# All experts' first matrices loaded at the end of the message stage, the chosen two copied by VectorE

## The chip, the core and the metric

The kernel runs on one core of a Trainium2 chip. The metric is the device time of one execution in microseconds (us), median of three runs. The core has five engines that run their own instruction queues and meet only at semaphores: TensorE (PE; its weight loads are PEld), VectorE (DVE), ScalarE (ACT), GpSimd (POOL) and SyncE (SP), which here does little but issue DMA transfers. Memory next to the engines is SBUF (128 partitions) and PSUM (eight banks for the sums of TensorE).

## What is computed

The input is a graph of 12500 nodes with 256 features and 212500 edges, sorted by target. The first half is one graph attention layer; the second, which the change touches, is a mixture of experts:

```python
def _L0_ffn_ref(x, Wr, br, W1, b1, W2, b2, gamma, beta):    # x: 1 x 12500 x 256
    logits = jnp.mean(x, axis=1) @ Wr + br                   # one row of 8 logits
    routing_weights = jax.nn.softmax(logits, axis=-1)
    ...                                                      # scaled by capacity, softmax again
    top_w, top_i = jax.lax.top_k(rw_tok, 2)
    top_w = jax.nn.softmax(top_w, axis=-1)
    h = gelu(einsum('nd,edf->enf', xf, W1) + b1)             # W1: 8 x 256 x 512
    y = einsum('enf,efd->end', h, W2) + b2                   # W2: 8 x 512 x 256
    out = einsum('ne,end->nd', w_dense, y)
    return _layer_norm(out + x, gamma, beta)
```

The mean over all nodes feeds the router, so all 12500 nodes get the same two experts of the eight. Which two is known only when the last node of the first half is done. The kernel then computes these two experts alone.

## The kernel before, in words

**Stages.** A first stage projects all rows and writes a table. The message stage (119 chunks of 1792 edges, with windows of 128 nodes) gathers rows of the table, forms messages and sums them by one-hot products on TensorE; for each window it stores the new rows (`x_mid`), their normalized form (`xn_rows`) and its transpose (`xn_cols`) to memory. Its last three steps are written out (`ahead_of_last`, `last`, `over_last`), and after them a short tail normalizes and stores the last window. Then comes the expert stage: 25 groups of 512 nodes (the last is short).

**The hand-over on VectorE** (lines 1838 to 1909). After the last window it adds up the column sums (`zcol`), TensorE multiplies them with Wr, and VectorE runs a chain of small operations on one partition: softmax, capacity, softmax again. Each is `link`ed: it raises the semaphore `s_setup` and waits for itself. At `N_PICKED` (line 1880) the indices of the two experts are in `top_ii`. It goes on with the weights of the two (lines 1881 to 1889, `N_TOP`; ScalarE does the exponentials, lines 1339 to 1341), TensorE spreads these over the partitions (line 1143) and VectorE copies them to `wtop`. Then it waits for W1 (line 1894), forms four combinations of W1's blocks (lines 1897 to 1900, `N_COMBOS`), waits for W2 and b2 (line 1902), and scales W2 and b2 with the weights (lines 1903 to 1908, `N_EXPERT`).

**The hand-over on SP** (lines 724 to 768). All its transfers go through one DMA queue (q1). It loads `x_mid` of groups 0 and 1 (`fx`), runs step `last`, waits for its sums, and loads `xn_cols` (as `fxT`) and `xn_rows` (as `fxn`) of both groups. Step `over_last` stores a window. Then:

```python
    sp.wait_ge(s_xn, (total + 2) * 32)      # line 739: all earlier stores of normalized rows have landed
    hold(sp, s_sp_held)
    store_xn(last, 0)                        # line 741
```

`hold` only raises a semaphore by one. Twelve more waits with a hold each follow (lines 742 to 751), for loads long done. Then SP waits for `N_PICKED`, reads the two indices into registers (line 753) and issues, for each expert, two halves of W1 and b1 (lines 757, 759), then for each W2 and b2 (lines 762, 764). Behind that it waits for the last stores (lines 765 to 768) and enters the loop over groups: load of group g+2, store of group g.

**A group** (TensorE from line 1058, ScalarE from 1345, VectorE from 1792 and 1806, POOL from 870). The first layer of a group is a 2x2 block product with seven instead of eight block products, in phases of four matmuls each (x8 instructions in the trace): P1 (line 1072), P2 (1074), P5 (1081), P6 (1085), P7 (1089), P4 (1093), P3 (1097). POOL forms the four combinations of the rows (`fx_c`, lines 878 to 883), VectorE once the four of the weights (`w1_c`). ScalarE copies partial sums to SBUF (lines 1352, 1355, 1358) and applies Gelu with the bias b1 (lines 1362, 1365, 1368, 1371). VectorE adds partial sums in `halves`: c11 after P2, c22 after P7, c12 after P3. The second layer is 64 instructions at line 1106; it waits for `N_EXPERT`. After it VectorE adds the input (`summed`, line 1812) and normalizes (`finished`).

TensorE runs the 24 full groups as a loop of four rounds of six (line 1145), ScalarE as a loop of two groups each; it waits for both b1 before it enters. POOL and VectorE have all groups written out.

**Where things lie.** In the expert stage the tiles of the message stage are used again: `fx`, `w1_sb`, `w2_sb`, `fo` (the output) and `fxT` are parts of `flat_rows`, the place of the gathered rows, which the trace therefore calls `rows`; `hT` and `fxn` are in `msg`, `w1_c` and `fx_c` in `oh`.

## Time and profile before

| | us |
|---|---|
| median of three runs (2863.31 to 2869.16) | 2867.67 |
| the profiled execution | 2866.4 |
| its span in the trace | 2864.6 |
| PE busy | 2295.6 (80%) |
| DVE busy | 2268.6 (79%) |
| ACT busy | 1927.5 (67%) |
| POOL busy | 1679.2 (59%) |

The span is the time between the first and the last instruction of the trace; all times in the text are counted from its start. The first stage ends near 150 us, the message stage near 2190, the expert stage fills the rest. Mean granted TensorE clock over the span: 0.907 of full. In rows from an engine's timeline the columns are start, duration, engine, line, operation, tiles written and read, number of instructions, and in brackets the idle time before with what ended it. SPq is SP's own queue, where DMA issues stand. The granted clock (PEclk) is 1.00 at 2.4 GHz and 0.50 at 1.2 GHz.

### The profile page before, as it was taken

The page shows a single profiled execution, that of the slowest core. Times are in us where ns is not written, and L with a number is a line of the kernel's source. Part 1 is how long each engine was busy: PE and PEld are TensorE (multiplying, and loading weights), DVE is VectorE, ACT ScalarE, POOL GpSimd, SP SyncE. Part 2 cuts the span into 40 slices and gives each one's busy share as a digit, 9 for nine tenths or more (in the row PEclk, how much of TensorE's full clock was granted, in tenths as well). Part 3 has the DMA queues.
Part 4 walks back from the last instruction along what each step waited for, and adds up shares of the span by engine and source line. Part 5 has one row for each costly group of instructions (what it writes and reads, how often), then busy time and mean ns, then how long its engine had stood idle before and what let it go on. Part 6 is the DMA issues. An engine that isn't in the chain of part 4 may idle for free. (4 is left out here: it accounts for less than half of the span.)

```text
span 2864.6 us, 56749 instructions
## 1 busy us (share of the span) xinstructions
PE 2295.6 (80%) x14050; PEld 1864.8 (65%) x14050; DVE 2268.6 (79%) x9465; ACT 1927.5 (67%) x6599; POOL 1679.2 (59%) x1771
## 2 busy tenths in 40 slices
PE   7846778777777778777777777778775999999998
PEld 5635656656656656656566656666664888888887
DVE  5538899899899989999899899899996465565566
ACT  4537778787787778777787787777784445445443
POOL 6767777777777777777777777777750111011110
PEclk9977898999888998989988998988897999999999
DMA  9977666666666666666666666666654122222222
GB/s 324 386 258 210 190 183 190 188 185 187 189 183 187 191 181 189 191 181 190 191 182 189 191 184 185 192 183 188 192 165 130 43 76 88 88 66 81 88 82 75
DMA packets 320818, 489.95 MB, mean 171 GB/s; under 512 B 74158, under 2 KB 226778, under 8 KB 320516
## 3 DMA queue, kind: packets, MB, share of 16 engines
q0 software_dynamic: 79760, 228.10, 30.3%
q1 hardware_dynamic: 240180, 257.44, 28.0%
q8 instruction: 100, 1.64, 0.2%
q14 instruction: 202, 1.65, 0.2%
q10 hardware_dynamic: 576, 1.12, 0.1%
HBM read 394.32 MB, written 92.15 MB: 170 GB/s over the span
## 5 line engine op out<-in xcount | busy, mean ns | idle before, releaser
L860 POOL DMA_INDIRECT rows<-table,idx x1543 | 1489.4, 965 | 481.3 <-issue 405.5
L963 PE MATMUL bank<-msg,oh 128*128 128x260 f32 x3324 | 858.1, 414 | 1.5 <-DVE acc L1703 1.2
L963 PEld LDWEIGHTS bank<-msg,oh 128*128 128x128 f32 x3324 | 678.7, 208 | 201.1 <-ACT xln L1318 23.0
L1210 ACT ACTIVATE msg<-rows,we 128x65 f32<-128x65 f32 x1888 | 474.8, 334 | 0.2
L1022 PE MATMUL bank<-ident_b,ohT 128*128 128x128 bf16 x1666 | 148.1, 257 | 313.0 <-DVE rden L1718 115.1
L1552 DVE TENSOR_TENSOR msg<-rows,bank 128x520 f32<-128x520 f32 x595 | 381.6, 679 | 0.5 <-DVEq L113 0.2
L878 POOL TENSOR_TENSOR oh<-rows 128x256 f32<-128x256 f32 x24 | 17.5, 730 | 593.3 <-PE bank L1093 507.4
L1022 PEld LDWEIGHTS bank<-ident_b,ohT 128*128 128x128 bf16 x1666 | 125.2, 116 | 327.4 <-DVE rden L1716 170.1
L1106 PE MATMUL bank<-rows,msg 128*128 128x256 f32 x1536 | 336.6, 378 | 0.0
L1106 PEld LDWEIGHTS bank<-rows,msg 128*128 128x128 f32 x1536 | 290.3, 189 | 42.4
L1249 ACT ACTIVATE asrc<-rows 128x70 f32<-128x70 f32 x119 | 31.8, 267 | 346.5 <-DMA rows<-table,idx 340.3
L1352 ACT ACTIVATE msg<-bank 128x256 f32<-128x256 f32 x96 | 36.6, 385 | 270.1 <-PE bank L1072 266.9
L1203 ACT ACTIVATE oh_b<-bank 128x896 bf16<-128x896 bf16 x238 | 203.3, 905 | 3.8 <-issue 3.4
L1203 ACT ACTIVATE oh<-bank 128x896 f32<-128x896 bf16 x238 | 201.1, 892 | 0.3 <-ACTq L113 0.2
L1658 DVE TENSOR_REDUCE node_v<-bank 128x70 f32<-128x210 f32 x119 | 44.8, 376 | 158.0 <-PE bank L985 143.3
L985 PE MATMUL bank<-ident,asrc 128*70 128x128 f32 x238 | 53.2, 307 | 143.5 <-ACT asrc L1249 125.9
L1547 DVE TENSOR_SCALAR ohT<-dst_b,node 128x896 bf16<-128x896 int16 x238 | 159.9, 672 | 1.2 <-DVEq L113 0.6
L985 PEld LDWEIGHTS bank<-ident,asrc 128*70 128x70 f32 x238 | 26.0, 144 | 186.1 <-ACT asrc L1249 170.8
L1001 PE MATMUL bank<-wx,xeT 128*128 128x260 f32 x480 | 144.8, 430 | 2.3 <-ACTq L113 1.4
L815 POOL DMA_INDIRECT rows<-in_x_rows,oh x119 | 114.4, 961 | 44.6 <-issue 22.5
L1304 ACT ACTIVATE selfm<-tab_w,ws 128x65 f32<-128x65 f32 x476 | 127.0, 338 | 3.9
L1267 ACT ACTIVATE r_c<-carry,r_f 1x65 f32<-1x65 f32 x476 | 125.1, 333 | 0.0
(250 smaller groups left out, 4876.1 us busy)
## 6 DMA issues: line engine op xcount, KB each, us to landing
dst_b<-dst SPq DMA_DIRECT2D x121, 448.0 KB
rows<-table,idx POOLq DMA_INDIRECT x1543
tab_w<-table SPq DMA_DIRECT2D x120, 134.5 KB
xe<-x_src SPq DMA_DIRECT2D x122, 128.0 KB
x_w<-in_x_rows SPq DMA_DIRECT2D x120, 128.0 KB
xn_rows<-xn SPq DMA_DIRECT2D x120, 128.0 KB
xn_cols<-xn_t SPq DMA_DIRECT2D x120, 128.0 KB
x_mid<-x_o SPq DMA_DIRECT2D x119, 128.0 KB
```

Source lines behind the costliest of these rows:

```text
L815: pool.indirect_dma_start(flat_rows[:, bass.ds(stage(c), D)], None, x, bass.IndirectOffsetOnAxis(ap=x_idx[:, c * TILES + GATHERS:(c + 1) * ...
L860: pool.indirect_dma_start(rows[0:n, slot, t, :], None, table, bass.IndirectOffsetOnAxis(ap=idx[slot][0:n, t:t + 1], axis=0), bounds_check= ...
L963: mm = pe.matmul(psA, oh[:, of, t, :], msg[:, of, t, :], start=(t == 0), stop=(t == TILES - 1))
L1001: mm = pe.matmul(psXR, xeT[:, k, :], wx[:, k, 0:D + H], start=(k == 0), stop=(k == KD - 1))
L1022: mm = pe.transpose(ps[:, c:c + P], ohT[:, s, t, 0:P], ident_b[:, :])
L1106: mm = pe.matmul(psY[q // 2][:, q % 2, :], hT[:, f, q * P:(q + 1) * P], w2_sb[:, e, fk, :], start=(f == 0), stop=(f == 2 * KF - 1))
L1203: ins = act.activation(to[:, i * half:(i + 1) * half, :], psO[i].rearrange("p (t n) -> p t n", n=P), ACT.Copy)
L1210: ins = act.activation(head_cols(msg[:, s, t, :])[:, h, :], head_cols(rows[:, at.slot(), t, 0:HC1])[:, h, :], ACT.Copy, scale=we[:, t, h:h ...
L1267: ins = act.activation(head_cols(r_c[:, :])[:, h, :], head_cols(carry[:, 0:HC1])[:, h, :], ACT.Copy, scale=r_f[:, h:h + 1])
L1304: ins = act.activation(head_cols(selfm[:, :])[:, h, :], head_cols(tab_w[:, at.slot(), 0:HC1])[:, h, :], ACT.Copy, scale=ws[:, h:h + 1])
L1547: return dve.tensor_scalar(ohT[:, s, t, 0:P], dst_b[:, s, :].rearrange("p (t n) -> p t n", n=P)[:, t, :], node[:, s:s + 1], None, ALU.is_e ...
L1552: mark(own, name, lambda: dve.tensor_tensor(msg[:, s, t:t + 2, :].rearrange("p t (h c) -> p t h c", h=H), rows[:, s4, t:t + 2, 0:HC1].rear ...
```

## The change

Five edits.

- **Place.** `w1_sb`, `w2_sb` and `fo` get SBUF of their own. In `flat_rows` there is now, behind `fx`, a tile `w1_all` for the first matrices of all eight experts (16 rows of 512 numbers in each partition, 4.19 MB in all), with `fxT` at the very end.
- **Load.** SP loads `w1_all` in one transfer right after the first `fxT` load, once VectorE and ScalarE have made their last messages (two waits are added for that), ahead of `fxn` of group 0 and of both loads of group 1. It is counted by one semaphore, `s_fw1`. The four loads of W1 halves after the picks are gone.
- **Copy.** At `N_PICKED` VectorE waits for the load, reads each index into a register and copies that expert's matrix to `w1_sb` (`N_CHOSEN`), then forms the four combinations. The weights chain (`N_TOP`) comes behind these.
- **Order in group 0.** TensorE no longer waits for `N_TOP` before the groups: the matmul that spreads the weights (`weights_out`, now into bank 7) stands in group 0 between P7 and P4. VectorE does c11 and c22 of group 0 (`halves_seen`) before it copies the weights and scales W2, and c12 (`halves_ended`) behind.
- **Loop.** TensorE's first six groups are written out, and the loop covers the other three rounds.

```diff
--- before.py
+++ after.py
@@ -315,15 +315,17 @@
         x_turn = -len(x_parts) % x_ring
         narrow = flat_rows[:, EP:2 * EP].bitcast(I16)[:, 0:EP]
         fx = part(flat_rows, 0, 3, QB, D)
-        w1_sb = part(flat_rows, slot_size, 2, KD, F)
-        w2_sb = part(flat_rows, slot_size + n_w, 2, KF, D)
-        fo = part(flat_rows, slot_size + 2 * n_w, 2, QB, D)
-        fxT = part(flat_rows, 3 * slot_size, 3, KD, GROUP)
+        n_all = NE * KD * F
+        w1_all = part(flat_rows, 3 * QB * D, NE, KD, F)
+        fxT = part(flat_rows, RING * slot_size - 3 * KD * GROUP, 3, KD, GROUP)
+        w1_sb = sb("w1_sb", [P, 2, KD, F])
+        w2_sb = sb("w2_sb", [P, 2, KF, D])
+        fo = sb("fo", [P, 2, QB, D])
         HG, PF = GROUP // 2, KF
         assert KD == 2 and KF % 2 == 0 and PF == 4
         w1_c = part(flat_oh, 0, 4, 2, KF // 2, P)
         fx_c = part(flat_oh, 4 * KF * P, 4, HG)
-        assert 3 * QB * D <= slot_size and slot_size + 2 * n_w + 2 * QB * D <= 3 * slot_size
+        assert 3 * QB * D + n_all <= RING * slot_size - 3 * KD * GROUP
 
 
         s_w = sem("s_w")
@@ -348,7 +350,7 @@
         s_mid = sem("s_mid")
         s_xn = sem("s_xn")
         s_fwr = sem("s_fwr")
-        s_fw1 = [[sem(f"s_fw1_{i}_{half}") for half in range(2)] for i in range(2)]
+        s_fw1 = sem("s_fw1")
         s_fb1 = sem("s_fb1")
         s_fw2 = sem("s_fw2")
         s_fx = [sem(f"s_fx{i}") for i in range(3)]
@@ -425,10 +427,11 @@
         N_SETUP = N_DIAG + 2
         N_MEAN = N_SETUP + 2 + 1
         N_PICKED = N_MEAN + 13
-        N_EXP = [N_MEAN + 3, N_PICKED + 2, N_PICKED + 7]
+        N_CHOSEN = [N_PICKED + 1, N_PICKED + 2]
+        N_COMBOS = N_PICKED + 6
+        N_EXP = [N_MEAN + 3, N_COMBOS + 2, N_COMBOS + 7]
         N_TOP = N_EXP[2] + 3
-        N_COMBOS = N_TOP + 5
-        N_EXPERT = N_COMBOS + 4
+        N_EXPERT = N_TOP + 5
         WTOP = 9
 
         pads = [(r, min(P, XO_ROWS - r)) for r in range(N, XO_ROWS, P)]
@@ -730,9 +733,16 @@
             step(last, -2, 0)
             pe2.wait(sp, "agg", last)
             hold(sp, s_sp_held)
-            for g in range(2):
-                load_cols(At(0, 3, 0), g)
-                load_rows(At(0, 3, 0), g, fxn, xn_rows)
+            load_cols(At(0, 3, 0), 0)
+            dve2.wait(sp, MSGS[-1], last)
+            hold(sp, s_sp_held)
+            act2.wait(sp, "msgs", last)
+            hold(sp, s_sp_held)
+            sp.dma_start(w1_all.rearrange("p e k f -> p (e k) f"),
+                         W1.rearrange("e (k p) f -> p (e k) f", p=P)).then_inc(s_fw1, 16)
+            load_rows(At(0, 3, 0), 0, fxn, xn_rows)
+            load_cols(At(0, 3, 0), 1)
+            load_rows(At(0, 3, 0), 1, fxn, xn_rows)
             step(over_last, -2, -1)
             fin_act.wait(sp, "nT", fin)
             hold(sp, s_sp_held)
@@ -752,10 +762,6 @@
             sp.wait_ge(s_setup, N_PICKED)
             picked = [sp.value_load(top_ii[0:1, i:i + 1], min_val=0, max_val=NE - 1) for i in range(2)]
             for i, e in enumerate(picked):
-                for half in range(2):
-                    f = slice(half * F // 2, (half + 1) * F // 2)
-                    sp.dma_start(w1_sb[:, i, :, f], W1[bass.ds(e, 1), :, f].rearrange("o (k p) f -> p (o k) f", p=P))\
-                      .then_inc(s_fw1[i][half], 16)
                 sp.dma_start(b1_sb[:, i, :], b1[bass.ds(e, 1), :].rearrange("o (k p) -> p (o k)", p=P),
                              allow_slow_non_contiguous=True).then_inc(s_fb1, 16)
             for i, e in enumerate(picked):
@@ -1055,7 +1061,7 @@
 
             pe3.credit(pe)
 
-            def group(at, at3):
+            def group(at, at3, between=None):
                 x0, x1 = [fxT[:, at3.slot(), k, 0:HG] for k in range(KD)], [fxT[:, at3.slot(), k, HG:] for k in range(KD)]
 
                 def block_of(i, k, m):
@@ -1068,7 +1074,7 @@
 
                 pe.wait_ge(s_fx[at3.slot()], at3.landed(3))
                 for m in range(PF):
-                    pe.wait_ge(s_fw1[m // 2][m % 2], 16)
+                    pe.wait_ge(s_setup, N_CHOSEN[m // (PF // 2)])
                     pe3.mark(f"P1_{m}", pe.matmul(psAl[m], block_of(0, 0, m), x0[0], start=True, stop=True))
                 for m in range(PF):
                     mm = pe.matmul(psBe[m // 2][:, m % 2, :], block_of(0, 1, m), x0[1], start=True, stop=True)
@@ -1088,6 +1094,8 @@
                     act3.wait(pe, f"u2_{m}", at)
                     pe3.mark(f"P7_{m}", pe.matmul(psAl[m], combo(2, m), fx_c[:, 2, :], start=False, stop=True,
                                                   skip_group_check=True))
+                if between:
+                    between()
                 for m in range(PF):
                     dve4.wait(pe, f"c22_{m}", at)
                     pe3.mark(f"P4_{m}", pe.matmul(psAl[m], block_of(1, 1, m), fx_c[:, 3, :], start=False, stop=True,
@@ -1139,10 +1147,13 @@
             for k in range(KD):
                 mm = pe.matmul(bank[4][0:1, 0:NE], zcol[:, k:k + 1], wr_sb[:, k, :], start=(k == 0), stop=(k == KD - 1))
             mm.then_inc(s_once, 1)
-            pe.wait_ge(s_setup, N_TOP)
-            pe.matmul(bank[5][:, 0:2], ones[0:1, :], rt[0:1, WTOP, 0:2], start=True, stop=True).then_inc(s_once, 1)
-            pe.wait_ge(s_setup, N_TOP + 1)
-            with pe.Fori(0, (GROUPS - 1) // 6) as k:
+            def weights_out():
+                pe.wait_ge(s_setup, N_TOP)
+                pe.matmul(psY[1][:, 0, 0:2], ones[0:1, :], rt[0:1, WTOP, 0:2], start=True, stop=True).then_inc(s_once, 1)
+
+            for j in range(6):
+                group(At(0, 2, j), At(0, 3, j), weights_out if j == 0 else None)
+            with pe.Fori(1, (GROUPS - 1) // 6) as k:
                 for j in range(6):
                     group(At(k * 3, 2, j), At(k * 2, 3, j))
             last_group(At(0, 2, GROUPS - 1), At(0, 3, GROUPS - 1))
@@ -1789,7 +1800,7 @@
                                                                      in1=ft[:, :], op0=ALU.add, op1=ALU.mult))
                     own(names[n + 2])
 
-            def halves(at):
+            def halves_seen(at):
 
                 for j in range(2):
                     pe3.wait(dve, f"P2_{j}", at)
@@ -1799,6 +1810,9 @@
                 for m in range(PF):
                     pe3.wait(dve, f"P7_{m}", at)
                     dve4.mark(f"c22_{m}", dve.tensor_tensor(hT[:, 2 * m + 1, HG:], psAl[m], hT[:, 2 * m + 1, HG:], ALU.add))
+
+            def halves_ended(at):
+
                 for m in range(PF):
                     pe3.wait(dve, f"P3_{m}", at)
                     dve4.mark(f"c12_{m}", dve.tensor_tensor(hT[:, 2 * m, HG:], psGa[m], hT[:, 2 * m, HG:], ALU.add))
@@ -1878,6 +1892,18 @@
             link(dve.max_index(top_i[:, :], rt[:, 8, :], rt[:, 6, :]))
             link(dve.tensor_copy(top_ii[:, :], top_i[:, :]))
             assert done[0] == N_PICKED
+            dve.wait_ge(s_fw1, 16)
+            for i in range(2):
+                e = dve.value_load(top_ii[0:1, i:i + 1], min_val=0, max_val=NE - 1)
+                link(dve.tensor_copy(w1_sb[:, i, :, :].unsqueeze(1), w1_all[:, bass.ds(e, 1), :, :]))
+                assert done[0] == N_CHOSEN[i]
+            a11, a12, a21, a22 = [w1_sb[:, :, k, :].rearrange("p e (h i f) -> p e h i f", i=2, f=P)[:, :, :, i, :]
+                                  for i in range(2) for k in range(KD)]
+            link(dve.tensor_tensor(w1_c[:, 0, :, :, :], a21, a22, ALU.add))
+            link(dve.tensor_tensor(w1_c[:, 1, :, :, :], w1_c[:, 0, :, :, :], a11, ALU.subtract))
+            link(dve.tensor_tensor(w1_c[:, 2, :, :, :], a11, a21, ALU.subtract))
+            link(dve.tensor_tensor(w1_c[:, 3, :, :, :], a12, w1_c[:, 1, :, :, :], ALU.subtract))
+            assert done[0] == N_COMBOS
             softmax(6, 7)
             link(dve.max(rt[:, 8, :], rt[:, 7, :]))
             link(dve.tensor_scalar(rt[:, 14, :], rt[:, 8, :], rt[:, 8, 0:1], None, ALU.subtract))
@@ -1887,18 +1913,9 @@
             link(dve.reciprocal(rt[:, 15, 2:3], rt[:, 15, 1:2]))
             link(dve.tensor_scalar(rt[:, WTOP, 0:2], rt[:, 13, 0:2], rt[:, 15, 2:3], None, ALU.mult))
             assert done[0] == N_TOP
+            halves_seen(At(0, 2, 0))
             dve.wait_ge(s_once, 6)
-            link(dve.tensor_copy(wtop[:, :], bank[5][:, 0:2]))
-            for e in range(2):
-                for half in range(2):
-                    dve.wait_ge(s_fw1[e][half], 16)
-            a11, a12, a21, a22 = [w1_sb[:, :, k, :].rearrange("p e (h i f) -> p e h i f", i=2, f=P)[:, :, :, i, :]
-                                  for i in range(2) for k in range(KD)]
-            link(dve.tensor_tensor(w1_c[:, 0, :, :, :], a21, a22, ALU.add))
-            link(dve.tensor_tensor(w1_c[:, 1, :, :, :], w1_c[:, 0, :, :, :], a11, ALU.subtract))
-            link(dve.tensor_tensor(w1_c[:, 2, :, :, :], a11, a21, ALU.subtract))
-            link(dve.tensor_tensor(w1_c[:, 3, :, :, :], a12, w1_c[:, 1, :, :, :], ALU.subtract))
-            assert done[0] == N_COMBOS
+            link(dve.tensor_copy(wtop[:, :], psY[1][:, 0, 0:2]))
             dve.wait_ge(s_fw2, 64)
             for i in range(2):
                 flat = w2_sb[:, i, :, :].rearrange("p k d -> p (k d)")
@@ -1915,7 +1932,9 @@
                 at = At(0, 2, g)
                 if g:
                     summed(*groups(g - 1), lambda: pe3.wait(dve, "out", at, -1))
-                halves(at)
+                if g:
+                    halves_seen(at)
+                halves_ended(at)
                 if g:
                     finished(*groups(g - 1))
             whole, short = groups(GROUPS - 2), groups(GROUPS - 1, QL)
```

## Rows read from the trace of the kernel before

**Rows 1.** The page: span, and busy time of each engine.

```profile
span 2864.6 us, 56749 instructions
...
PE 2295.6 (80%) x14050; PEld 1864.8 (65%) x14050; DVE 2268.6 (79%) x9465; ACT 1927.5 (67%) x6599; POOL 1679.2 (59%) x1771
```

**Rows 2.** The chain of waits around group 0: start us, us, what.

```profile
2200.74 0.28 SPq L753
...
2207.60 6.44 DMA b_sb<-in_L_ffn_b
...
2222.39 13.86 PE bank L1106 x64
```

**Rows 3.** The chain of waits in a steady group.

```profile
2265.66 1.73 PE bank L1081 x8
...
2269.55 1.28 ACT L1362
...
2274.96 13.86 PE bank L1106 x64
```

**Rows 4.** ScalarE in order of time, group 0.

```profile
2209.25 1.28 ACT L1352 ACT_TABLE_LOAD   x1 [9.25 <-DMA b_sb<-in_L_ffn_b]
```

**Rows 5.** VectorE in order of time, picks and weights.

```profile
2197.79 0.16 DVE L1879 CAST top_ii<-top_i 1x8 int32<-1x8 uint32 x1
...
2208.79 0.69 DVE L1897 TENSOR_TENSOR oh<-rows 128x512 f32<-128x512 f32 x1 [7.21 <-DMA rows<-in_L_ffn_W]
...
2214.14 1.54 DVE L1905 TENSOR_SCALAR rows<-rows,wtop 128x1024 f32<-128x1024 f32 x2 [2.47 <-DMA b_sb<-in_L_ffn_b]
```

**Rows 6.** TensorE in order of time, group 0.

```profile
2209.81 3.28 PE L1074 MATMUL bank<-rows 128*128 128x256 f32 x8
2212.93 1.89 PE L1081 MATMUL bank<-oh 128*128 128x256 f32 x8
```

**Rows 7.** SP's DMA issues in order of time.

```profile
2183.34 0.40 SPq L715 DMA_DIRECT2D rows<-xn_cols  x1
...
2184.87 0.47 SPq L710 DMA_DIRECT2D msg<-xn_rows  x1
2191.26 0.36 SPq L643 DMA_DIRECT2D x_mid<-x_o  x1
...
2193.51 1.60 SPq L613 DMA_DIRECT2D xn_cols<-xn_t  x1
2197.68 0.33 SPq L612 DMA_DIRECT2D xn_rows<-xn  x1
...
2202.04 1.00 SPq L757 DMA_DIRECT2D rows<-in_L_ffn_W  x2
2203.22 0.37 SPq L759 DMA_DIRECT2D b_sb<-in_L_ffn_b  x1
...
2204.88 0.37 SPq L759 DMA_DIRECT2D b_sb<-in_L_ffn_b  x1
```

**Rows 8.** One-microsecond stretches; the heading row names the columns.

```profile
core 0: us, PE busy (x) PEld busy (x) DVE busy (x) ACT busy (x) POOL busy (x), PEclk, DMA share, GB/s
...
2189.00:2190.00 1.00, 0.00 (x0) 0.00 (x0) 0.73 (x3) 0.00 (x0) 0.00 (x0) 0.50 1.05 397
...
2195.00:2196.00 1.00, 0.00 (x0) 0.00 (x0) 0.59 (x4) 0.21 (x1) 0.92 (x3) 0.50 0.34 105
...
2210.00:2211.00 1.00, 1.00 (x4) 0.82 (x3) 0.93 (x3) 0.99 (x3) 0.00 (x0) 0.50 0.85 256
...
2212.00:2213.00 1.00, 1.00 (x5) 0.86 (x4) 0.00 (x0) 0.00 (x0) 0.00 (x0) 0.69 0.92 229
```

**Rows 9.** Landing: fxT issued 2183.34, fxn issued 2184.87, both b1.

```profile
DMA to landing us min/median/max: 5.1/5.1/5.1
...
DMA to landing us min/median/max: 8.0/8.0/8.0
...
DMA to landing us min/median/max: 3.9/4.0/4.2
```

## The prediction, made before the change was run

> **What bounds the kernel now.** I read the page first [rows 1]: no engine is full over the span, so the chain that ended last has to be read stage by stage. The change touches only the hand-over between the message stage and the expert stage, some 40 us of 2864.6. There the chain of waits [rows 2] goes: SP reads the two picked experts at 2200.74, issues their loads, the last of them (b2, issued 2207.60) lands 6.44 us later, and the second layer of group 0 starts at 2222.39. From there to the end it is TensorE without a gap that the change could touch; steady groups have the same chain as group 0, with 9.30 us from P5 (2265.66) to the second layer (2274.96) in the groups where ScalarE swaps its table [rows 3]. So everything is decided by when group 0's second layer starts: 2222.39 plus or minus.
>
> Three things hold group 0 today. TensorE's first product waits for the first W1 half. ScalarE starts only when both b1 vectors have landed: it sits until 2209.25, loads its table for 1.28 us and copies [rows 4]. VectorE adds up its combinations at 2208.79 and scales W2 from 2214.14 [rows 5]. TensorE does P2 in 3.28 us at the half clock and P5 at 2212.93 [rows 6]. SP's queue in the same stretch is [rows 7]; how fast the transfers flow is in the one-microsecond stretches [rows 8], and when they land in [rows 9].
>
> **The change, part by part.**
>
> *Removed:* four W1 issues of SP between the picks and b1. From the first (2202.04) to b1 of that expert (2203.22) is 1.18 us, so twice 1.18 = 2.4 us less ahead of the second b1. Also 1.05 MB less in front of b1, b2 and W2.
>
> *Added on the queue:* one load of 4.19 MB, issued right after the first fxT load of 2183.34, and three loads of 0.52 MB (fxn of group 0, fxT and fxn of group 1) behind it instead of ahead. SP adds two waits that are long fulfilled (VectorE's last messages ended near 2171) and one issue, under 1 us; nobody waits for SP there, since its next work is the x_mid store at 2191.26 [rows 7].
> Price of the load: the first fxT landed at 2183.34 + 5.1 = 2188.4 and the last fxn at 2184.87 + 8.0 = 2192.9 [rows 7, 9], so 1.57 MB took 4.4 us, 355 GB/s, and in the full microsecond 2189 it was 397 GB/s [rows 8]. Between these I take 380 for long rows: 4.19 MB = 11.0 us (11.8 to 10.6). W1 lands at 2188.4 + 11.0 = 2199.4, the last fxn at 2203.9.
> The Trainium skill ("DMA: Bandwidth & Descriptors", section Bandwidth) measures 425 GB/s on a 16 MB load. By that the load would take 9.9 us and the sum would be 1.1 us lower; no row here shows more than 397 over a microsecond.
>
> *VectorE:* the picks are ready at 2197.95 [rows 5], so W1 is awaited 1.5 us. Then twice a register load (SP's takes 0.28 [rows 2], about 0.55 with its checks) and a copy of 128x1024. The trace has no such copy: the W2 scaling does the same size in 0.77 [rows 5]; the bound above is twice that. That gives 2199.4 + 2 x 1.35 = 2202.1, the four combinations at 0.72 end at 2205.0 [rows 5], the moved weights chain at 2207.7 (an estimate of 2.7 us: before, it fitted between the picks at 2197.95 and SP's reading at 2200.74). All of it lies before ScalarE starts, so it costs nothing; if that cover went, it would be the 2205.0 that gates P5. W2's scaling, moved behind group 0's P7 additions, takes 2.4 us beside P4 and P3 (3.5 us), and is hidden too. The spreading matmul moved into group 0 is two tiny instructions, at most 0.6 us at the half clock, in a gap before P4. POOL's four subtractions wait for fxn of group 0 at about 2200.9 and need 2.7 us: hidden.
>
> *Moved, and on the path: SP's wait for its stores.* This is the term that decides. Before it may store the last normalized rows (line 741) SP waits for all stores of the step before (line 739). Those are issued at 2191.26 to 2193.51 on the same queue [rows 7]. Before, they met a nearly empty queue and the last was done by about 2197.0, so the store at 2197.68 followed. Now they stand behind the whole backlog: it lands at 2203.9, its data are through some 1.4 us earlier, the 0.39 MB of stores need 1.3 us at 105 GB/s per 0.34 share [rows 8], and the receipt 0.6: 2204.4, the store of line 741 at 2205.1, 7.4 us later. Behind it in SP are twelve waits with their holds (3.06 us from 2197.68 to the pick at 2200.74 [rows 7, 2]), the picks, b1, W2. So the second b1 is issued at 2204.88 + 7.4 - 2.4 = 2209.9. It lands 4.0 us after its issue (3.9 to 4.2 [rows 9]): ScalarE starts at 2214.1 instead of 2209.25, its table and first copy take 1.28 + 0.4, and P5 starts at 2215.8 instead of 2212.93. W2 is issued from 2210.5 to 2212.7 and lands by 2218.7, before VectorE wants it near 2223.
>
> *Clock.* TensorE was granted the half clock from 2186 until the stretch 2212, where it rose (0.69 in that microsecond) after some 4 us of unbroken work that began near 2208.8 [rows 8]. There the slow time lay under waiting. Now P1 and P2 run near 2200 to 2207, TensorE then idles for 9 us, and P5 and a part of P6 meet the half clock: 4 us of work that would be 2 us, so +1.9 us (bounds 0 and 3.5).
>
> *Six groups written out:* TensorE's loop of four rounds becomes one written out and three. The back edges between rounds show no gap in the chain, nor is the loop's entry on the path; nothing, with 0.5 us either way.
>
> *Sum:* P5 at 2215.8, plus 9.30, plus 1.9 = 2227.0 against 2222.39: +4.6 us. On the profiled execution of 2866.4 us that is 2871.0; the median of the three timed runs, 2867.67, stands 1.3 us higher, so I forecast 2872. A measurement of this kernel can tell about 0.2% (5.7 us) from no change; the sum lies inside.
>
> **Rivals.**
>
> *A. The stores are not held up (the other side).* If the three small stores pass the backlog, line 741 stays at 2197.68. The second b1 is issued at 2202.5 and lands at 2206.6, P5 comes at 2208.4 and the second layer at 2217.7 to 2219.6 depending on the clock: -3.7 us, 2864. With the clock's 1.9 us the second layer starts at 2219.6 plus the hold-up of line 741, so this rival decides where that hold-up is under 2.8 us, line 741 before 2200.5. For it: 2.4 us of issues are gone. Against it: the loads landed in the order of their issue [rows 9], all on one queue. The Trainium skill ("DMA: Bandwidth & Descriptors", section Queues, rings and completion order) says that a later descriptor may finish its write before an earlier one, while starts are in ring order. By the first half of that the gain of 3.7 us would be had; the landings here bear out the second half.
>
> *B. The big load flows slowly.* W1's rows stand 256 KB apart in each partition. Mixed traffic moved 256 GB/s at 0.85 share at 2210 [rows 8]; at 300 GB/s the load takes 14.0 us (+3.0), at 256 16.4 us (+5.4). All terms shift with it: +7.6 to +10.0 us, 2875 to 2878. For it speaks only that the loads of 2184 began slowly, against it the 397.
>
> *C. The load is hidden and the path moves little.* If SP's own pace after the wait is shorter without W1 in front of b1 (3 us to land instead of 4) and the clock rises while P1 and P2 run and holds, 1 + 1.9 us fall away: +1.7 us, 2869.
>
> **How the numbers follow.** Held stores at the expected rate: 0.6, with its own range of +1 to +8 us, about a third of it above 5.7. A: 0.17, of which about a third could read as a gain over 0.2%. B: 0.15, nearly all slower. C: 0.08. Slower by over 0.2%: 0.6 x 0.35 + 0.14, with the uncertainty of the medians 0.36; faster by over 0.2%: 0.07; within: 0.57. Range 2863 to 2879: it takes in A's centre below and B's slow end above.
>
> **What would show it.** Right: the store of line 741 near 2205 and a wait of SP for xn_cols of 6 us or more before it; ScalarE's first table load near 2214; W1 landing about 15 us after its issue; P5 at the half clock; the second layer of group 0 near 2227, and all later groups shifted alike. Wrong: line 741 still at 2197.7 (A), W1 landing after 2203 (B), a group 0 that waits for VectorE's copies or combinations, or any change inside the later groups or the message stage.

## The result and the profile after

Twelve runs of each kernel on the same chip gave medians of 2865.96 us before and 2870.52 us with the change, 4.6 us slower: 1.0017 times as long, with a 95% interval of 1.0010 to 1.0024. One of the runs before fell in the chip's slower state and took 3597.61 us; the ratio leaves it out, and without it the median before is 2865.66 us and the difference 4.9 us. The forecast was 2872 us in a range of 2863 to 2879, with "within 0.2%" as the likeliest outcome.

The profiled execution of the changed kernel took 2870.95 us. The page begins so; it answers to [rows 1], and no engine's busy time moved by more than 6 us:

```profile
span 2869.1 us, 56593 instructions
...
PE 2297.0 (80%) x14050; PEld 1870.5 (65%) x14050; DVE 2274.5 (79%) x9467; ACT 1926.5 (67%) x6599; POOL 1684.5 (59%) x1771
```

The span is 4.5 us longer. To place them I measure from a common point, **the turning**: TensorE's matmuls that turn the last normalized rows, at the end of the message stage. They start at 2192.44 before and at 2193.41 after. So 0.97 us arose earlier. Of these, 0.88 us are there before the change can act: SP's last `x_mid` store ahead of the big load goes out at 2180.46 before and at 2181.34 after. From the turning to the second layer of group 0, both by TensorE's order in time, it is 29.79 us before and 34.08 after: +4.29. From there to the end it is 642.37 and 641.61: -0.76. The three make 4.5 us. "Offset" below is always time since the turning.

SP's DMA issues in order of time, changed kernel (it answers to [rows 7]):

```profile
2184.95 0.38 SPq L741 DMA_DIRECT2D rows<-in_L_ffn_W  x1
2185.37 6.12 SPq L713 DMA_DIRECT2D msg<-xn_rows  x1
2191.54 2.60 SPq L718 DMA_DIRECT2D rows<-xn_cols  x1
2194.18 1.31 SPq L713 DMA_DIRECT2D msg<-xn_rows  x1
2196.64 0.89 SPq L646 DMA_DIRECT2D x_mid<-x_o  x1
...
2199.26 0.39 SPq L616 DMA_DIRECT2D xn_cols<-xn_t  x1
2206.55 0.33 SPq L615 DMA_DIRECT2D xn_rows<-xn  x1
...
2210.89 1.00 SPq L765 DMA_DIRECT2D b_sb<-in_L_ffn_b  x2
```

The store that was on line 741 before (now `store_xn` at 2206.55) comes 13.14 us after the turning instead of 5.24: it was held 7.9 us. What held it stands in the table of waits of SP, changed kernel (engine and line, what was waited for, us in total, times, longest), and the landing of the big load in the view of line 741:

```profile
SPq L456 <- DMA xn_cols<-xn_t: 5.9, 1, 5.9
```

```profile
DMA to landing us min/median/max: 15.4/15.4/15.4
```

The load issued at 2184.95 landed at 2200.35. The three loads behind it kept the DMA engines busy until 2205; the last of them, issued at 2194.18, landed 10.4 us later, at 2204.58. One-microsecond stretches (columns as in [rows 8]):

```profile
2191.00:2192.00 1.00, 0.00 (x0) 0.00 (x0) 0.82 (x3) 0.00 (x0) 0.00 (x0) 0.50 1.05 410
2197.00:2198.00 1.00, 0.00 (x0) 0.00 (x0) 0.86 (x6) 0.00 (x0) 0.00 (x0) 0.50 1.03 381
2203.00:2204.00 1.00, 1.00 (x4) 0.34 (x2) 0.97 (x2) 0.00 (x0) 1.00 (x2) 0.50 1.10 365
2204.00:2205.00 1.00, 1.00 (x3) 0.82 (x3) 1.00 (x1) 0.00 (x0) 0.92 (x2) 0.50 0.55 165
2205.00:2206.00 1.00, 1.00 (x4) 0.81 (x3) 0.96 (x2) 0.00 (x0) 0.67 (x1) 0.50 0.01 4
2206.00:2207.00 1.00, 1.00 (x4) 0.82 (x3) 0.93 (x3) 0.00 (x0) 0.00 (x0) 0.50 0.00 0
2207.00:2208.00 1.00, 1.00 (x6) 0.81 (x5) 0.93 (x3) 0.00 (x0) 0.00 (x0) 1.00 0.39 135
2210.00:2211.00 1.00, 0.00 (x0) 0.00 (x0) 0.37 (x2) 0.00 (x0) 0.00 (x0) 0.71 0.00 0
2219.00:2220.00 1.00, 1.00 (x3) 0.77 (x3) 0.00 (x0) 0.38 (x1) 0.00 (x0) 0.50 0.96 344
2220.00:2221.00 1.00, 1.00 (x5) 0.82 (x4) 0.00 (x0) 0.40 (x2) 0.00 (x0) 0.67 1.06 384
```

The DMA share is full until 2204 and next to empty from 2205; SP is released at 2205.75 (2199.26 + 6.49 in the chain below) and issues its store at 2206.55. The clock reached full speed at 2207, while P1 and P2 ran, and was back at the half clock from 2211, after TensorE had gone idle. The chain of waits around group 0, changed kernel (it answers to [rows 2]):

```profile
2199.26 6.49 DMA xn_cols<-xn_t
...
2211.50 2.14 DMA b_sb<-in_L_ffn_b
...
2215.64 3.75 PE bank L1087 x8
2219.39 2.42 PE bank L1091 x8
2221.81 1.73 PE bank L1095 x8
2223.53 0.31 PE bank L1152 x2
...
2227.66 13.81 PE bank L1114 x64
```

Ahead of this piece the chain runs through SP's own issues, the 6.12, 2.60 and 1.31 us above; then come the very stores that SP waits for. The loads of the chosen matrices are gone from it. L1087 is P5 and L1091 is P6; in the next group they take 1.73 and 1.74 us. And VectorE in order of time:

```profile
2201.23 0.69 DVE L1898 COPY w_sb<-rows 128x1024 f32 x1 [3.02 <-DMA rows<-in_L_ffn_W]
2202.71 1.23 DVE L1898 COPY w_sb<-rows 128x1024 f32 x1 [0.79 <-DVE w_sb L1898]
2203.97 1.11 DVE L1902 TENSOR_TENSOR oh<-w_sb 128x512 f32<-128x512 f32 x1
...
2206.98 0.69 DVE L1905 TENSOR_TENSOR oh<-w_sb,oh 128x512 f32<-128x512 f32 x1
```

The first matrices are ready for TensorE earlier than before (combinations done at offset 14.3 against 19.2). P1 and P2 use that, and then TensorE has to stop: P5 needs ScalarE's first copies, and ScalarE is without b1.

### The profile page after: what moved, and what is told of

It reads as the page before. It is cut to its first block and busy times, and to the rows that moved or that the text cites. A ratio compares the mean times of both kernels' runs of the same rounds, so it can differ in the third digit from the quotient of the medians.

```text
span 2869.1 us, 56593 instructions
## 1 busy us (share of the span) xinstructions
PE 2297.0 (80%) x14050; PEld 1870.5 (65%) x14050; DVE 2274.5 (79%) x9467; ACT 1926.5 (67%) x6599; POOL 1684.5 (59%) x1771
## 5 line engine op out<-in xcount | busy, mean ns | idle before, releaser
L1114 PE MATMUL bank<-w_sb,msg 128*128 128x256 f32 x1536 | 335.4, 379 | 0.0
L1114 PEld LDWEIGHTS bank<-w_sb,msg 128*128 128x128 f32 x1536 | 291.8, 190 | 39.7
```

Source lines behind the costliest of these rows:

```text
L1114: mm = pe.matmul(psY[q // 2][:, q % 2, :], hT[:, f, q * P:(q + 1) * P], w2_sb[:, e, fk, :], start=(f == 0), stop=(f == 2 * KF - 1))
```

## The experiments

They ran on other chips, on which the message stage is longer (3280 and 3330 us for the kernel before), so each ratio is against the kernel before on the same chip, and offsets are from each run's own turning.

**1. The picks ahead of the wait for the stores.** SP reads the picks and issues b1, W2 and b2 before the last two stores.

```diff
             step(over_last, -2, -1)
...
+            sp.wait_ge(s_setup, N_PICKED)
+            picked = [sp.value_load(...) for i in range(2)]
+            ... b1, W2, b2 ...
             sp.wait_ge(s_xn, (total + 2) * 32)
             store_xn(last, 0)
-            sp.wait_ge(s_setup, N_PICKED)
-            picked = [sp.value_load(...) for i in range(2)]
-            ... b1, W2, b2 ...
```

> The changed kernel, but SP reads the picks and issues b1, W2 and b2 before it waits for the stores of the last-but-one window. Theory (SP is held at that wait by stores that stand behind the W1 backlog on its queue): the second b1 is issued near 2201.7 instead of 2211.5 and lands behind the backlog near 2206, ScalarE's first table load falls from 2213.8 to about 2206.5, P5 from 2215.6 to about 2208.3, the second layer of group 0 from 2227.7 to about 2218: 9 to 10 us less than the changed kernel, some 5 us less than the kernel before (2861). Rival (the volume on the transfer engines delays b1 wherever it is issued): b1 lands near 2213 again and the time stays within 2 us of 2870.5.

Measured: 1.0003 of the kernel before [0.9994, 1.0012]. b1 is issued at offset 7.9 instead of 17.5 and the second layer starts at 29.13 instead of 34.08: 4.95 us come back, more than the 4.29 that were lost, and the median is that of the kernel before (3280.66 and 3280.65 us): SP's picks behind that wait cost as much as the whole loss. The other half of the 9 to 10 us that I expected did not come. ScalarE in order of time, this kernel:

```profile
2621.64 0.21 ACT L1352 ACTIVATE rt<-rt 1x8 f32<-1x8 f32 x1 [12.18 <-DVE rt L1876]
2623.01 0.21 ACT L1352 ACTIVATE rt<-rt 1x8 f32<-1x8 f32 x1 [1.17 <-DVE rt L1909]
2623.26 1.28 ACT L1363 ACT_TABLE_LOAD   x1
```

The table load has no wait for b1 any more; it comes right behind the exponentials of the router's weights, and these stand behind VectorE's copies and combinations. The change had moved that chain back, and this is the next thing to be late. (Run 11 tests it.)

**2. The same order in the kernel before.** The same edit, made to it.

> The kernel before, with the same reordering of SP alone (W1 halves, b1, W2, b2 before the wait for the stores). Theory: nothing holds that wait there, so only SP's own 2.7 us between the picks (2197.95) and the first W1 issue (2202.04) go: 2 to 3 us less than before, 2863. Rival (the reordering is worth the same with and without the large load): as much as in the run beside it, 9 us.

Measured: 1.0003 [0.9994, 1.0012], second layer at 28.99. The 2 to 3 us that I expected did not come, and still less the rival's 9. SP's first W1 issue did move from offset 9.60 to 6.82, but ScalarE's table load only from 16.81 to 15.36, since b1 took 3.9 to 5.5 us to land. In the kernel before, SP's order costs nothing that shows in the time: its wait for the stores is 1.6 us.

**3. The big load on ScalarE's queue.** Issued by ScalarE behind its last messages, at offset -13.1 instead of -8.5.

```diff
-            sp.dma_start(w1_all..., W1...).then_inc(s_fw1, 16)
...
             step(last, -2, 0, late=LAST_LATE)
+            dve2.wait(act, MSGS[-1], last)
+            act2.wait(act, "msgs", last)
+            act.dma_start(w1_all..., W1...).then_inc(s_fw1, 16)
```

> The changed kernel with the W1 load issued by ScalarE on its own queue, after its last messages; SP's order unchanged. Theory (it is the order within SP's queue that holds the stores): SP's issues no longer stall for 6.1, 2.6 and 1.3 us, the stores of the last-but-one window are issued near 2194 and landed by about 2200, the last store goes out near 2200 instead of 2206.5, b1 lands near 2207; W1 itself lands later, near 2204 instead of 2200.4, since both queues share the engines, and then gates: P5 near 2212, second layer near 2222, 4 to 6 us less than the changed kernel. Rival (the engines are simply full until 2204.6, whichever queue): last store near 2206, no gain over 2 us.

Measured: 1.0000 [0.9991, 1.0009], second layer at 30.89, 3.2 us less than with the change: less than the 4 to 6 us of my theory, more than the 2 us of the rival. SP's own issues are quicker again (0.61, 1.25 and 1.53 us), but the wait for its stores is as long as ever. SP's waits; three of SP's issues; the loads with their size and median us from issue to landing; and a one-microsecond stretch (the turning is at 2604.97):

```profile
SPq L456 <- DMA xn_cols<-xn_t: 6.8, 1, 6.8
```

```profile
2599.15 1.53 SPq L713 DMA_DIRECT2D msg<-xn_rows  x1
...
2607.24 0.39 SPq L616 DMA_DIRECT2D xn_cols<-xn_t  x1
2615.33 0.33 SPq L615 DMA_DIRECT2D xn_rows<-xn  x1
```

```profile
rows<-in_L_ffn_W ACTq DMA_DIRECT2D x1, 4096.0 KB, 18.4
rows<-xn_cols SPq DMA_DIRECT2D x2, 512.0 KB, 12.3
msg<-xn_rows SPq DMA_DIRECT2D x2, 512.0 KB, 13.9
```

```profile
2613.00:2614.00 1.00, 1.00 (x3) 0.50 (x3) 0.96 (x2) 0.00 (x0) 0.92 (x2) 0.50 0.29 84
```

The stores, issued by 2607.24 on SP's queue, were not seen complete until everything had passed at 2613.3; the last store follows at offset 10.36. Without a backlog it would have come at about 6.4, an estimate: the `xn_cols` store went out at 2.27, and in the kernel before the last store followed 4.17 us behind that one. What held them is seen in the landings. The big load, issued at 2591.88, had landed at 2610.3. But SP's own last three loads, ahead of the stores on the same queue, took 13.5, 14.2 and 14.3 us one by one and landed at 2610.7, 2612.1 and 2613.5, in the order of their issue; in the kernel before they took 6.4, 7.0 and 8.0. So the big load held the stores by slowing what stood before them on their own queue. The experiment does not show what stores on an otherwise empty queue would do; none was run. The load began 4.6 us earlier and all transfers were through 2.9 us earlier, which is about the gain of 3.2 us; nothing is left over that the other queue brought. The Trainium skill ("DMA: Bandwidth & Descriptors", section Issuing engines are not separate DMA queues) says that transfers of all issuing engines run on the same 16 DMA engines and interleave; SP's loads, at 13.5 to 14.3 us beside the other queue's, agree.

**4. TensorE kept busy.** Sixteen more matmuls between P2 and P5 of group 0, into a bank that is free then.

```diff
+                for i in range(filler):
+                    pe.matmul(psY[0][:, 0, :], block_of(0, 0, i % PF), x0[0], start=True, stop=True)
                 pool3.wait(pe, "T4", at)
```

> The changed kernel with 16 matmuls of 128x256 more in group 0 between P2 and P5, into a bank that the second layer clears; they add nothing to the result. They fill 6.9 of the 7.3 us in which TensorE idles before P5. Theory (P5 and a part of P6 run at the half clock because TensorE has idled): P5 takes 1.7 instead of 3.75 us and P6 1.7 instead of 2.4, 2.7 us less than the changed kernel, 2867.8. Rival (the clock does not hold over such filling, or ScalarE's copies set P5's pace): no change, or up to 0.5 us more.

Measured: 1.0034 [1.0021, 1.0047], slower than the changed kernel (1.0017, and 1.0020 in run 5). Yet the clock's part was as foreseen: P5 took 1.97 us, and from P5 to the second layer it was 9.37 us instead of about 12. The time went elsewhere. The chain of waits of this kernel, some 300 us later, and TensorE in order of time, later still:

```profile
2928.21 13.81 PE bank L1116 x64
2942.02 3.36 issue
2945.38 3.34 PE bank L1078 x8
```

```profile
3107.36 1.89 PE L1078 MATMUL bank<-rows,w_sb 128*128 128x256 f32 x8 [2.97 <-issue]
```

Where the loop over the remaining groups goes round, TensorE stood 3.0 to 3.4 us with nothing to wait for, once with P1 at the half clock behind it; from the second layer of group 0 to the end it was 649.17 us instead of 641.6. In the changed kernel the only such gap is 0.30 us. So the 7.6 us seem to belong to the loop and not to the clock; runs 9 and 10 test that.

**5. The changed kernel once more,** unchanged, beside the next three.

> The changed kernel as it is, on the chip on which the experiments run, where the message stage takes some 410 us longer. All theories: counted from TensorE's turning of the last window's normalized rows (2192.44 before, 2193.41 after in the first traces), the second layer of group 0 starts about 34.1 us later (35 where the transfers are a little slower, as in the run with the filling), against 29.8 for the kernel before; in time 4 to 5 us more than the kernel before.

Measured: 1.0020 [1.0011, 1.0028]; second layer at 34.44, the rest 641.43. The loss is that of the first chip, within the intervals; the medians are 6.9 us apart.

**6. Writing out alone.** The kernel before with its first six groups written out.

```diff
-            with pe.Fori(0, (GROUPS - 1) // 6) as k:
+            for j in range(6):
+                group(At(0, 2, j), At(0, 3, j))
+            with pe.Fori(1, (GROUPS - 1) // 6) as k:
```

> The kernel before with TensorE's first six groups written out and the loop over the other three rounds; nothing else. Theory (that part of the change is worth nothing, since TensorE crosses its back edges without a gap): same as before within 1 us, second layer 29.8 us after the turning of the last rows. Rival (where the loop's body lies decides whether a back edge stalls, as the run with the filling showed with 3.4 and 3.0 us at two of them): no change in group 0, but 3 us or more at one or more back edges.

Measured: 1.0003 [0.9995, 1.0012], and no gap at a back edge of more than 0.3 us. This part costs nothing that shows. The last store is at offset 4.14 and the second layer at 27.96, 1.8 us earlier than in the profile of the kernel before. In the profile of the kernel before, the issue at 2193.51 had taken 1.60 us [rows 7], in this one 0.39; so that profile seems to have had about a microsecond of bad luck in the stretch I priced.

**7. Half the load.** Only experts 1 to 4 are read (2.10 MB); both experts that this input picks are among them.

```diff
-            sp.dma_start(w1_all.rearrange(...), W1.rearrange(...))
+            sp.dma_start(w1_all[:, 1:5, :, :].rearrange(...), W1[1:5, :, :].rearrange(...))
```

> The changed kernel, but the load covers experts 1 to 4 alone (2.10 MB instead of 4.19); the two picked ones of this input are among them. Theory (backlog on SP's queue holds the stores): at 385 GB/s the backlog is 5.4 us shorter, so SP's last store goes out 7.7 us after the turning of the last rows instead of 13.1, and the second layer starts 5 to 5.5 us earlier than in the changed kernel, about 0.5 to 1 us earlier than in the kernel before. Rival (a fixed cost of the copies or of SP's order): less than 2 us of gain.

Measured: 0.9998 [0.9989, 1.0006]. The last store comes at 8.11 instead of 13.32 and the second layer at 30.15 instead of 34.44. 2.10 MB less took 5.2 us out of the store's time (5.4 expected), which is 403 GB/s. Of these, 4.3 us reached the second layer, where I had expected 5 to 5.5. SP's issues behind the shorter load:

```profile
2657.79 0.38 SPq L741 DMA_DIRECT2D rows<-in_L_ffn_W  x1
2658.22 0.57 SPq L713 DMA_DIRECT2D msg<-xn_rows  x1
2658.84 2.61 SPq L718 DMA_DIRECT2D rows<-xn_cols  x1
...
2674.19 0.33 SPq L615 DMA_DIRECT2D xn_rows<-xn  x1
```

The hold-up of the store thus follows the size of the load, byte for byte. P5 still takes 3.75 us, since TensorE idles all the same (4.03 us).

**8. All three repairs:** load on ScalarE's queue, picks first, and the weights' chain ahead of VectorE's wait for W1.

```diff
             link(dve.tensor_copy(top_ii[:, :], top_i[:, :]))
+            ... weights' chain (softmax, max, sum, reciprocal) ...
             dve.wait_ge(s_fw1, 16)
             ... two copies, four combinations ...
-            ... weights' chain ...
```

> The changed kernel with W1 loaded by ScalarE's queue, SP's picks, b1, W2 and b2 ahead of its wait for the stores, and VectorE's weights chain ahead of the wait for W1 and the copies. Theory (the hold-up of SP, and ScalarE's waiting for exponentials behind the combinations, are what kept the first two variants from gaining): ScalarE starts when b1 lands, P5 follows P2 without an idle stretch about 14 us after the turning of the last rows with the clock just up, second layer at 23.5 to 25 us instead of 29.8 before: 5 to 6 us less than the kernel before. Rival (P1 and P2 at the half clock and the copies set the pace whatever SP does): 28 to 29 us, within 1.5 us of the kernel before.

Measured: 0.9985 [0.9976, 0.9994], 5.5 us less than the kernel before in medians, with the second layer at 24.69. The table load came at offset 9.61.

**9 and 10. Without the loop.** The changed kernel with all groups of TensorE written out, and the same with the sixteen matmuls of run 4.

```diff
-            for j in range(6):
+            for j in range(GROUPS - 1):
                 group(At(0, 2, j), At(0, 3, j), weights_out if j == 0 else None)
-            with pe.Fori(1, (GROUPS - 1) // 6) as k:
-                ...
```

> The changed kernel with all 24 full groups of TensorE written out, no loop. Control for the next run. Theory (back edges of this loop cost 0.3 us at most in the changed kernel): within 1 us of the changed kernel, so 4 to 7 us more than the kernel before, ratio 1.0015 to 1.002. From the second layer of group 0 to the end about 641.3 us. Rival (written-out code has to be fetched all along and stalls now and then): more than 642 us there.

> The same with the 16 filling matmuls between P2 and P5 of group 0. Theory (the stalls of 3.4 and 3.0 us at two back edges of the filling run came from where the loop's code lay, and the filling itself saves the half clock in P5 and P6): no stall marked issue after group 0, 641.3 us from its second layer to the end as in the control, and 2.5 us less than the control in time. Rival (the stalls come from the filling in another way, or the clock is paid back later): stalls of 3 us again, or a half-clock stretch in a later group, and no gain over the control.

Measured: 1.0015 [1.0006, 1.0024] and 1.0007 [0.9998, 1.0016]. Neither has a gap of TensorE in the groups (the rest is 641.05 and 641.09 us), and the matmuls now bring the second layer from 34.37 to 31.63. In medians, 3286.32 and 3284.11, that is 2.2 us, but the two intervals overlap, so the gain rests on the traces. TensorE in order of time, with the matmuls (L1084):

```profile
2626.52 7.07 PE L1084 MATMUL bank<-rows,w_sb 128*128 128x256 f32 x32
2633.94 1.97 PE L1089 MATMUL bank<-oh 128*128 128x256 f32 x8 [0.35 <-ACT msg L1362]
```

So the clock costs the changed kernel some 2.7 us, and the loss of run 4 came with the loop: the same matmuls without it lose nothing.

**11. Picks first and weights early,** with the load left on SP's queue.

> The changed kernel with two of the three edits of the fastest run: SP's picks, b1, W2 and b2 ahead of its wait for the stores, and VectorE's weights chain ahead of its wait for W1 and the copies; W1 still goes through SP's queue. Theory (in the run with the picks first, ScalarE was held by the exponentials behind the combinations, not by b1): ScalarE starts when b1 lands, near 12 us after the turning of the last rows instead of 16.5; P5 follows the combinations and P2, near 16; second layer near 26.5, that is 2.5 us less than with the picks first alone and 1.5 to 2 us more than with all three. Rival (W1's landing and the copies beside POOL set P5): second layer at 28.5 or later.

Measured: 3276.88 against 3281.01 us, 0.9986 [0.9977, 0.9995]; second layer at 24.64. ScalarE and TensorE in order of time:

```profile
2619.26 1.28 ACT L1363 ACT_TABLE_LOAD   x1 [6.60 <-DMA b_sb<-in_L_ffn_b]
```

```profile
2615.04 3.81 PE L1078 MATMUL bank<-rows,w_sb 128*128 128x256 f32 x8 [7.51 <-DVE w_sb L1907]
2618.64 2.25 PE L1080 MATMUL bank<-rows,w_sb 128*128 128x256 f32 x8
2621.09 1.97 PE L1087 MATMUL bank<-oh 128*128 128x256 f32 x8 [0.19 <-ACT msg L1363]
```

I had expected 26.5. But P5 follows P2 with 0.19 us of idling at 2621.09, so the clock that P1 and P2 raised is kept (P5 takes 1.97 us) and the 2.7 us of its loss are gone too, without any matmul added. It does as well as run 8 with two edits of SP's and VectorE's order, and it beats both kernels: 4.1 us less than the one before, and 9.4 less than the changed one of run 9.

## Why the prediction came out right, point by point

**The store of the last rows** was the term that decides, and it was right in kind and size: 7.4 us of hold-up predicted, 7.9 measured, with SP's wait for `xn_cols` of 5.9 us in front of it ("6 us or more" was asked). Less the 0.97 us by which the stretch began late, the store came at 2205.6 (2205.1 predicted) and the second b1 at 2210.5 (2209.9). The half microsecond is the last piece: from the last load's landing (2204.58) to SP's release (2205.75) it was 1.2 us, where the sum has 0.5. Run 7 shows that the hold-up scales with the bytes, run 1 that it costs the whole loss. Rival A, stores that pass the backlog, is refuted by the store's time itself, and in run 3 SP's queue kept its order beside another queue's load.

One step of this part was wrong, "nobody waits for SP there": its three loads behind the big one took 10.0 us to issue instead of 1.5, so the `x_mid` store left at 2196.64, 4.4 us late by the offset, and the `xn_cols` store at 2199.26, 4.8 us late. That cost nothing more, because the stores had to wait until the backlog was through in any case: in run 7 the `x_mid` store left on time (offset -1.19), in run 3 the three issues took 3.4 us, and the last store was late in both.

**The load** landed at 2199.4 by the same reckoning (2199.4 predicted), at 381 to 410 GB/s in each full microsecond from 2189 to 2199 (the range of 355 to 397 that I had taken ended a little low). Rival B, a slow flow over the 256 KB pitch, is refuted.

**b1's flight was mis-sized.** I carried 4.0 us over from [rows 9], where b1 had W1 loads about it. On queues that had just run empty it landed in 2.14 us, so ScalarE began at 2212.85 (2214.1 predicted). Rival C had named this half; its other half, a clock that holds, did not come.

**The clock was mis-sized the other way.** The mechanism was right: the clock rose in P2 (2207), fell in the 7.3 us of idling and left P5 and P6 with 3.75 and 2.42 us instead of 1.73 each, 2.7 us where I took 1.9. I had misread where TensorE's unbroken work before the rise began in the kernel before: at 2207.95, not near 2208.8. TensorE in order of time there:

```profile
2207.95 2.08 PE L1072 MATMUL bank<-rows 128*128 128x256 f32 x4 [0.98 <-DMA rows<-in_L_ffn_W]
```

So I counted 4 us of P5 and P6 at the half clock, and it was 5 (2215.64 until the stretch 2220). With the spreading matmul, 0.31 us (bound 0.6), from P5 to the second layer it took 12.0 us against 11.2. That stayed below the bound of 3.5 us; run 10 gets the 2.7 us back.

The two errors, -1.9 and +0.8, and the +0.6 on SP's path largely cancel, so the second layer is at 2226.7 (2227.0 predicted) and the sum at +4.3 instead of +4.6. A part of the agreement is luck, and so is that the medians differ by just 4.6 us: between the profiles 0.97 us came from ahead of the stretch and 0.76 went behind it, neither of them in the sum. The forecast's 2872 started from a median of three, 2867.67, which lies 1.7 us above that of twelve.

**VectorE's cover was thinner than I wrote.** The combinations ended at 2206.7 (2205.0 predicted) and the weights' chain at 2209.4 (2207.7), since the second copy and two combinations ran beside POOL and took 1.23 and 1.11 us. That left 3.4 us before ScalarE's start. I had priced the moved chain at nothing, rightly for this kernel, but named only the 2205.0 as what comes late next; in run 1 it was ScalarE's exponentials, the last of which began 0.25 us ahead of its table load.

**Writing out six groups** cost nothing that shows (run 6), as put down, but the bound of half a microsecond either way was too narrow for what a loop can do: run 4 lost 7.6 us.

**From the second layer on** it took 0.76 us less. Each block of 64 matmuls lasts 13.81 us in the chain, not 13.86, in every kernel with the change that has been profiled, which over 24 blocks is 1.2 us. A difference at hand is that its weights come from a buffer of their own; the cause was not tested. I had said that any change inside the later groups would speak against the theory; this one is small and goes the other way.

The real loss is perhaps a little larger than the pair of profiles shows. From run 6 to run 5, on one chip, the second layer moves by 34.44 - 27.96 = 6.5 us and the last store by 13.32 - 4.14 = 9.2 us instead of 7.9; the medians differ by 7.0 us. The intervals of both comparisons, 1.0010 to 1.0024 and 1.0011 to 1.0028, hold 4.6 and 6.5 us alike, so this stays open.

## What to carry to other kernels

A prefetch is not free because it is early: small stores that somebody waits for completed only when the bulk issued before them was through, and moving the bulk to another queue did not free them while other loads stood ahead of them on their own. So take what matters (here b1, and the picks it needs) out from behind that wait, as run 1 and run 11 did, or make the load smaller (run 7); putting the bulk load behind the last such store was not tried; ask of every wait that is shortened what stood next in line on each engine, since here three things (b1, the exponentials, the clock) ended within a few microseconds of each other and a gain over the kernel before came only when all were moved (runs 8 and 11).

## What the runs showed of the hardware that I had not expected

- SP's next issues behind the 4.19 MB load took 6.12, 2.60 and 1.31 us instead of 0.4 to 0.5 [rows 7]; behind 2.10 MB, 0.57, 2.61 and 1.98. With the load on ScalarE's queue they took 0.61, 1.25 and 1.53. So SP itself stood while the backlog was long, and x_mid's store was issued 4.4 us later (offset 3.23 instead of -1.18).
- Beside POOL's `TENSOR_TENSOR`, VectorE's f32 copy of 128x1024 took 1.23 us instead of 0.69, its `TENSOR_TENSOR` 1.11 instead of 0.69, and POOL's own 1.18 instead of 0.72. In runs 7 and 8, where POOL had ended first, all of VectorE's took 0.69 or 0.70. POOL in order of time, changed kernel, beside the copies and combinations shown above:

```profile
2203.35 1.18 POOL L887 TENSOR_TENSOR oh<-rows,oh 128x256 f32<-128x256 f32 x1
```

  The Trainium skill ("SBUF — State Buffer", section SBUF: two separate sides) tells of a port that the two engines share and hold in turn, one blocked until the other's instruction ends; that both sides lengthened, each by less than one instruction of the other, agrees with it.
- TensorE stood 3.36 and 2.97 us where its loop goes round, in the one kernel with sixteen more matmuls written ahead of the loop; in the changed kernel it is 0.30 us, and without the loop (runs 9 and 10) nothing. What decides it stays open.
- The 512 four-byte rows of b1 landed in 2.1 us when nothing was under way ahead of them, in 3.9 to 4.2 behind other loads [rows 9].
